# Bias and mask rows split on 80 partitions and stacked through a DRAM scratch, with the first tanh ahead of them

## The reference, cut to what matters

```
# 1 gated convolution, 7 taps, depthwise
gate = sigmoid(conv(x, gate_w) + gate_b);  cand = tanh(conv(x, cand_w) + cand_b)
h    = decay_scan(gate * cand);  y = h @ out_w.T + out_b + x;  y = rmsnorm(y) * norm_w
x    = layernorm(x + y)
# 2 cross attention, 16 heads of 8, causal, with an additive mask of the keys
wq = q @ Wq + bq;  wk = ctx @ Wk + bk;  wv = ctx @ Wv + bv
scores = where(causal, wq . wk / sqrt(8), min) + mask
x    = layernorm(x + softmax(scores) @ wv @ Wp + bp)
# 3 mixture of experts: gate, up and down, each routed to the top 2 of 8 experts
x    = layernorm(x + moe(silu(moe(x)) * moe(x)))
```

## Time and profile before

| | |
|---|---|
| time, median of 3 runs | 298.7 us (297.55 to 301.46) |
| the profiled execution's own time | 298.14 us |
| its span, first to last instruction | 296.4 us |
| mean granted TensorE clock | 0.936 |
| busy: PE, PEld, DVE, ACT, POOL | 257.1, 188.2, 190.8, 82.2, 111.1 us |
| mean DMA rate over the span | 79 GB/s |

### The profile page before, as it was taken

One profiled execution on the slowest core, in us unless ns is written; L12 is line 12 of the kernel. 1 busy time (PEld: TensorE's weight loads), 2 busy tenths in 40 slices (PEclk: granted clock), 3 DMA queues, 4 the chain that ended last, 5 costly groups with the idle time before them and its releaser, 6 DMA issues.

```text
span 296.4 us, 4809 instructions
## 1 busy us (share of the span) xinstructions
PE 257.1 (87%) x1756; PEld 188.2 (63%) x1756; DVE 190.8 (64%) x563; ACT 82.2 (28%) x157; POOL 111.1 (37%) x131
## 2 busy tenths in 40 slices
PE   6669857856986959999999999999999999999992
PEld 3546433425664737776777777777777787787871
DVE  5587862768697376556972884497188458566365
ACT  2424337135424201332133043114304313131000
POOL 4025329579314812048119205600930361070001
PEclk9997968995798885999999999999999999999997
DMA  5913625337420000262013005300300400320000
GB/s 192 380 50 112 197 75 148 116 106 214 160 71 1 3 0 0 109 209 77 0 48 107 2 0 170 125 0 13 142 2 1 155 0 2 71 81 9 2 0 18
DMA packets 12982, 23.48 MB, mean 79 GB/s; under 512 B 1584, under 2 KB 7824, under 8 KB 12954
## 3 DMA queue, kind: packets, MB, share of 16 engines
q1 hardware_dynamic: 11950, 22.17, 22.5%
q10 hardware_dynamic: 1008, 1.01, 1.0%
HBM read 19.81 MB, written 4.42 MB: 82 GB/s over the span
## 4 chain that ended last, share of the span: by engine, by line
PE 44%; DVE 31%; issue 12%; POOL 7%; ACT 3%; DMA 2%; SPq 1%; POOLq 0%; DVEq 0%; ACTq 0%
PE PS L1115 19%; PE PS L1167 8%; DVE NM L1321 4%; DVE ROOM L1454 3%; PE PS L1036 3%; PE PS L1047 2%; DMA PT<-aux 2%; DVE XL L1403 2%; PE PS L1050 2%; POOL PT L665 2%; DVE WL L1209 2%; PE PS L1010 2%; PE PS L881 2%; PE PS L1005 1%; PE PS L1089 1%
## 5 line engine op out<-in xcount | busy, mean ns | idle before, releaser
L1115 PE MATMUL PS<-WH,XH 128*128 128x512 f32 x128 | 57.8, 452 | 0.0
L1115 PE MATMUL PS<-WL,XH 128*128 128x512 f32 x128 | 52.2, 408 | 0.0
L1115 PE MATMUL PS<-WH,XL 128*128 128x512 f32 x128 | 52.2, 408 | 0.0
L689 POOL TENSOR_TENSOR ROOM<-ROOM,X2T 128x512 f32<-128x512 f32 x24 | 31.3, 1335 | 10.3 <-DMA ROOM<-CGD 10.3
L665 POOL TENSOR_SCALAR_AFFINE_SELECT PT<-PT 128x1024 f32<-128x1024 f32 x16 | 18.4, 1147 | 31.3 <-ACT PT L796 31.3
L1115 PEld LDWEIGHTS PS<-WH,XL 128*128 128x128 f32 x128 | 25.0, 196 | 6.1
L1115 PEld LDWEIGHTS PS<-WH,XH 128*128 128x128 f32 x128 | 25.1, 196 | 5.4 <-issue 0.4
L1115 PEld LDWEIGHTS PS<-WL,XH 128*128 128x128 f32 x128 | 25.2, 197 | 3.5 <-issue 0.2
L1167 PE MATMUL PS<-WH,ITH 128*128 128x512 f32 x56 | 23.7, 423 | 0.0
L607 POOL TENSOR_SCALAR R<-M 128x1 f32<-128x1 f32 x8 | 1.5, 190 | 58.0 <-DVE M L1467 58.0
L881 PE MATMUL PS<-XT,DIAG 128*128 128x256 f32 (+1 forms) x56 | 22.3, 538 | 0.0
(11 more groups left out here) (182 smaller groups left out, 491.8 us busy)
## 6 DMA issues: line engine op xcount, KB each, us to landing
ROOM<-CGD SPq DMA_DIRECT2D x12, 512.0 KB, 4.4
ROOM<-w_gate SPq DMA_DIRECT2D x4, 512.0 KB, 8.1
ROOM<-w_up SPq DMA_DIRECT2D x4, 512.0 KB, 4.5
ROOM<-w_down SPq DMA_DIRECT2D x4, 512.0 KB, 4.5
KD<-LOW SPq DMA_DIRECT2D x6, 256.0 KB, 4.4
KS<-KD SPq DMA_DIRECT2D x3, 512.0 KB, 3.6
QS<-QD SPq DMA_DIRECT2D x3, 512.0 KB, 4.5
QD<-LOW SPq DMA_DIRECT2D x3, 256.0 KB, 3.8
```

Of the source, the lines that this page charges most:

```text
L689: g.tensor_tensor(cb, cb, X2T[:, None, :].broadcast_to([P, 4, P]), ALU.mult).then_inc(f_xe, 1)
L1115: last = mm(PS[:, product_bank(t, r), :], a[:, r, cut], w[:, r, e * I:(e + 1) * I], start=e == 0 and n == 0, stop=e == E - 1 and n == 2)
```

## The change

The five rows are folded: 2048 columns are 16 pieces of 128, so 5 rows become 80 partitions of 128 columns. SP loads them so, now third, ahead of RO. ScalarE makes two results of 80 partitions by 128 columns (the scaled rows, and their low parts, with the choice of rows in the scale column), VectorE subtracts once. SP's new first step AX stores the result to the DRAM tensor AD, waits for the store, and loads the first 1280 columns of its five rows into AUX. K 0 waits for that load. VectorE's MX is gone, and SP's MX copies the masks from AD to MD, in DRAM. ScalarE's and VectorE's lists have GT 0 ahead of AX.

```diff
-C_AM = C_AW + 1
-C_BK, C_BQ = C_AM + 1, C_AM + 2
+C_BK, C_BQ = C_AW + 1, C_AW + 2
+A_FOLD = (A_T + M_COLS) // P
...
+        AD = nc.dram_tensor("AD", (A_ROWS, A_FOLD * P), F32, kind="Internal").ap()
...
-        AUX_RAW = PT[0:A_ROWS, :, :, :].rearrange("p a b c -> p (a b c)")
-        AUX_LOW = XH[0:A_ROWS, :, :].rearrange("p a b -> p (a b)")
-        MASKS = XL[0:A_ROWS, 0, :]
+        FOLD_RAW, FOLD_ALL = PT[0:A_ROWS * A_FOLD, 0, 0, :], PT[0:A_ROWS * A_FOLD, 0, 1, :]
+        FOLD_LOW, FOLD = XH[0:A_ROWS * A_FOLD, 0, 0:P], XH[0:A_ROWS * A_FOLD, 0, P:2 * P]
...
+            sp.dma_start(FOLD_RAW, aux.rearrange("a (c j) -> (a c) j", j=P)).then_inc(ld_a, 16)
             sp.dma_start(RO[:, :], rows.partition_broadcast(P)).then_inc(ld_r, 16)
-            sp.dma_start(AUX_RAW, aux).then_inc(ld_a, 16)
...
+                elif what == "AX":
+                    sp.wait_ge(c_aux, 3)
+                    sp.dma_start(AD.rearrange("a (c j) -> (a c) j", j=P), FOLD.bitcast(F32)).then_inc(st_a, 16)
+                    sp.wait_ge(st_a, 16)
+                    sp.wait_ge(c_id, 6)
+                    sp.dma_start(AUX[0:A_ROWS, :].bitcast(F32), AD[:, 0:A_COLS]).then_inc(ld_aux, 16)
                 elif what == "MX":
-                    sp.wait_ge(c_aux, 5)
-                    sp.dma_start(MD[0:2], MASKS[3:5, :].bitcast(F32)).then_inc(st_m, 16)
-                    sp.dma_start(MD[2:4], MASKS[0:2, :].bitcast(F32)).then_inc(st_m, 16)
+                    sp.wait_ge(c_id, 6)
+                    sp.dma_start(MD[0:2], AD[3:5, A_T:]).then_inc(st_m, 16)
+                    sp.dma_start(MD[2:4], AD[0:2, A_T:]).then_inc(st_m, 16)
...
-                    aux_q = AUX_RAW[:, A_Q:A_T]
-                    s.activation(aux_q, aux_q, ACT.Copy, scale=CO[0:A_ROWS, C_AS:C_AS + 1]).then_inc(c_aux, 1)
-                    s.activation(AUX_LOW[:, A_T:A_T + M_COLS], AUX_RAW[:, A_T:A_T + M_COLS], ACT.Copy,
-                                 scale=CO[0:A_ROWS, C_AM:C_AM + 1]).then_inc(c_aux, 1)
-                    act.wait_ge(c_aux, 1)
-                    s.activation(AUX_LOW[:, 0:A_T], AUX_RAW[:, 0:A_T], ACT.Copy,
-                                 scale=CO[0:A_ROWS, C_AW:C_AW + 1]).then_inc(c_aux, 1)
+                    s.activation(FOLD_ALL, FOLD_RAW, ACT.Copy, scale=CO[0:A_ROWS * A_FOLD, C_AS:C_AS + 1])\
+                        .then_inc(c_aux, 1)
+                    s.activation(FOLD_LOW, FOLD_RAW, ACT.Copy, scale=CO[0:A_ROWS * A_FOLD, C_AW:C_AW + 1])\
+                        .then_inc(c_aux, 1)
...
                         pe.wait_ge(ld_k, NLK)
-                        pe.wait_ge(c_aux, 4)
+                        pe.wait_ge(ld_aux, 16)
...
-                    dve.wait_ge(c_aux, 3)
-                    dve.wait_ge(c_id, 6)
-                    v.tensor_tensor(AUX[0:A_ROWS, :], AUX_RAW[:, 0:A_COLS], AUX_LOW[:, 0:A_COLS].bitcast(F32), ALU.subtract)\
-                        .then_inc(c_aux, 1)
-                elif what == "MX":
-                    dve.wait_ge(c_aux, 4)
-                    v.tensor_tensor(MASKS, AUX_RAW[:, A_T:A_T + M_COLS], AUX_LOW[:, A_T:A_T + M_COLS].bitcast(F32),
-                                    ALU.subtract).then_inc(c_aux, 1)
+                    dve.wait_ge(c_aux, 2)
+                    v.tensor_tensor(FOLD, FOLD_ALL, FOLD_LOW.bitcast(F32), ALU.subtract).then_inc(c_aux, 1)
...
+    row_of, part = np.arange(P) // A_FOLD, np.arange(P) % A_FOLD * P
+    scales = np.where((row_of < 2) & (part >= A_Q) & (part < A_T), np.float32(SCALE), np.float32(1))
+    lows = (row_of == np.where(part < A_T, 1, 4)).astype(np.float32)
...
+        scales[:, None], (scales * lows)[:, None],
```

More of the change, by code:

```diff
@@ L61 @@
 MASK_HI, MASK_LO, MAX_HI, MAX_LO = range(COPIES - 1, 4 * COPIES, COPIES)
-EARLY = {'PE': [('WM', 4), ('WM', 1), ('WM', 1), ('GC', 0), ('GC', 1), ('O', 0), ('C1', 0), ('KN', 0), ('K', 0), ('X1', 0), ('C1', 1), ('V', 0), ('KN', 1), ('Q', 0), ('V', 1), ('C1', 2), ('S', 0, 0), ('O', 1), ('S', 0, 1), ('C1', 3), ('C1', 4), ('A', 0), ('X1', 1), ('ST', 0, 0), ('ST', 0, 1), ('C1', 5), ('C1', 6), ('PV', 0, 0), ('C1', 7), ('PV', 0, 1), ('WO', 0), ('S', 1, 0), ('C1', 8), ('C1', 9), ('X2', 0), ('QN', 0), ('LG', 0), ('C1', 10), ('C1', 11), ('C1', 12), ('C1', 13), ('S', 1, 1), ('T', 0), ('T', 1), ('A', 1)], 'ACT': [('AX',), ('GT', 0), ('O', 0), ('KE', 0), ('X1', 0), ('KN', 0), ('W', 0), ('GT', 1), ('QE', 0), ('W', 1), ('KN', 1), ('O', 1), ('X1', 1), ('W', 2), ('W', 3), ('ST', 0, 0), ('ST', 0, 1), ('DC',), ('W', 4), ('W', 6), ('X2', 0), ('LG', 0), ('QN', 0), ('W', 5), ('T', 0), ('T', 1), ('W', 7)], 'DVE': [('GC', 0), ('AX',), ('GT', 0), ('GC', 1, 0), ('GC', 1, 1), ('O', 0), ('GC', 1, 2), ('QW',), ('GC', 1, 3), ('N1', 0), ('N1A', 0), ('GC', 1, 4), ('GC', 1, 5), ('GC', 1, 6), ('N1B', 0), ('KE', 0), ('KN', 0), ('GT', 1), ('V', 0), ('MX',), ('QE', 0), ('KN', 1), ('WL', 1, 0), ('O', 1), ('S', 0, 0), ('S', 0, 1), ('N1', 1), ('N1A', 1), ('V', 1), ('NM', 0), ('A', 0), ('N1B', 1), ('WL', 1, 1), ('RD',), ('WL', 3, 1), ('WL', 3, 0), ('PV', 0, 1), ('WO', 0), ('N2', 0), ('S', 1, 0), ('LG', 0), ('WL', 5, 1), ('T', 0), ('QN', 0), ('S', 1, 1), ('NM', 1), ('A', 1), ('T', 1)], 'POOL': [('GT', 0), ('N1', 0), ('N1B', 0), ('WL', 0, 0), ('GT', 1), ('WL', 0, 1), ('VM', 0), ('N1', 1), ('N1B', 1), ('WL', 2, 1), ('X1', 0), ('WL', 2, 0), ('ST', 0, 0), ('X1', 1), ('ST', 0, 1), ('WL', 4, 1), ('N2', 0), ('WL', 6, 0), ('WL', 6, 1), ('WL', 4, 0), ('XE', 0), ('XE', 1), ('XE', 2), ('WL', 5, 0), ('XE', 3), ('WL', 7, 1), ('VM', 1), ('WL', 7, 0)], 'SP': [('KN', 0), ('W', 0), ('MX',), ('MS',), ('W', 1), ('W', 3), ('W', 2), ('KN', 1), ('W', 4), ('QN', 0), ('W', 5), ('W', 6)]}
@@ new lines @@
+EARLY = {'PE': [('WM', 4), ('WM', 1), ('WM', 1), ('GC', 0), ('GC', 1), ('O', 0), ('C1', 0), ('KN', 0), ('K', 0), ('X1', 0), ('C1', 1), ('V', 0), ('KN', 1), ('Q', 0), ('V', 1), ('C1', 2), ('S', 0, 0), ('O', 1), ('S', 0, 1), ('C1', 3), ('C1', 4), ('A', 0), ('X1', 1), ('ST', 0, 0), ('ST', 0, 1), ('C1', 5), ('C1', 6), ('PV', 0, 0), ('C1', 7), ('PV', 0, 1), ('WO', 0), ('S', 1, 0), ('C1', 8), ('C1', 9), ('X2', 0), ('QN', 0), ('LG', 0), ('C1', 10), ('C1', 11), ('C1', 12), ('C1', 13), ('S', 1, 1), ('T', 0), ('T', 1), ('A', 1)], 'ACT': [('GT', 0), ('AX',), ('O', 0), ('KE', 0), ('X1', 0), ('KN', 0), ('W', 0), ('GT', 1), ('QE', 0), ('W', 1), ('KN', 1), ('O', 1), ('X1', 1), ('W', 2), ('W', 3), ('ST', 0, 0), ('ST', 0, 1), ('DC',), ('W', 4), ('W', 6), ('X2', 0), ('LG', 0), ('QN', 0), ('W', 5), ('T', 0), ('T', 1), ('W', 7)], 'DVE': [('GC', 0), ('GT', 0), ('AX',), ('GC', 1, 0), ('GC', 1, 1), ('O', 0), ('GC', 1, 2), ('QW',), ('GC', 1, 3), ('N1', 0), ('N1A', 0), ('GC', 1, 4), ('GC', 1, 5), ('GC', 1, 6), ('N1B', 0), ('KE', 0), ('KN', 0), ('GT', 1), ('V', 0), ('QE', 0), ('KN', 1), ('WL', 1, 0), ('O', 1), ('S', 0, 0), ('S', 0, 1), ('N1', 1), ('N1A', 1), ('V', 1), ('NM', 0), ('A', 0), ('N1B', 1), ('WL', 1, 1), ('RD',), ('WL', 3, 1), ('WL', 3, 0), ('PV', 0, 1), ('WO', 0), ('N2', 0), ('S', 1, 0), ('LG', 0), ('WL', 5, 1), ('T', 0), ('QN', 0), ('S', 1, 1), ('NM', 1), ('A', 1), ('T', 1)], 'POOL': [('GT', 0), ('N1', 0), ('N1B', 0), ('WL', 0, 0), ('GT', 1), ('WL', 0, 1), ('VM', 0), ('N1', 1), ('N1B', 1), ('WL', 2, 1), ('X1', 0), ('WL', 2, 0), ('ST', 0, 0), ('X1', 1), ('ST', 0, 1), ('WL', 4, 1), ('N2', 0), ('WL', 6, 0), ('WL', 6, 1), ('WL', 4, 0), ('XE', 0), ('XE', 1), ('XE', 2), ('WL', 5, 0), ('XE', 3), ('WL', 7, 1), ('VM', 1), ('WL', 7, 0)], 'SP': [('AX',), ('KN', 0), ('W', 0), ('MX',), ('MS',), ('W', 1), ('W', 3), ('W', 2), ('KN', 1), ('W', 4), ('QN', 0), ('W', 5), ('W', 6)]}
@@ L323, in decoder_layer @@
         c_aux = sem("c_aux")
+        st_a = sem("st_a")
+        ld_aux = sem("ld_aux")
         dv = sem("dv")
@@ L1504 @@
         marks(*range(2, 32, COPIES)), marks(*range(1, 32, COPIES), MASK_LO),
-        np.where(np.arange(P) < 2, np.float32(SCALE), np.float32(1))[:, None],
-        (np.arange(P) == 1).astype(np.float32)[:, None],
-        (np.arange(P) == 4).astype(np.float32)[:, None],
+        scales[:, None], (scales * lows)[:, None],
         a["L0_xattn_bk"][:, None], a["L0_xattn_bq"][:, None]], axis=1)
```

## The result

The changed kernel takes 300.58 us (median of 20 runs, 298.33 to 303.87) where the kernel before, in 20 runs beside them, takes 300.38 (295.76 to 303.34). The ratio is 1.0089, with a 95% interval of 1.0051 to 1.0128: slower by 0.9%. This ratio leaves out the runs more than 1.5% above the fastest of their kernel, 11 of the 20 before and 5 of the 20 after; the means of all 20 are 299.72 and 301.18 us, 0.5% apart (0.1 to 0.9%). So the runs show that the change costs time, and its size only as somewhere between 0.1 and 1.3%. The profiled execution took 299.41 us, span 297.7, against 298.14 and 296.4 before. Two repeats gave 1.0066 (1.0026 to 1.0107), and a median of 301.95 against 300.9. The means of all runs of the three comparisons together, 40 of the changed kernel and 52 of the kernel before, put the cost at 1.6 us, give or take 0.8.

The account below looks back on a forecast made before the run. The prediction took the chain of waits to belong to TensorE for 44% and VectorE for 31%, transfers 2%. Terms of +3.5, -0.6 and -0.3 gave +2.6 on the profiled 298.14: 300.7 us, range 295.6 to 303.0.

Parts of the forecast that it names:

- GT 0 ahead: At the head, the first tanh starts at about 8.5 us, O 0 runs 2.6 us earlier, norms end 2.7 earlier.
- Work on 80 partitions: Two ScalarE operations of 0.3 us and a VectorE one of about 0.3; result ready for the store at 10.9.
- The round trip: Store and reload ahead of K 0: store waits behind weight loads, seen at 17.5, AUX lands at 19.5 us.
- the estimate of 20.2: End of store and reload in us, at about 2.0 us fixed per transfer; not the figure the forecast used.
- The clock in K 0: After TensorE's idle stretch K 0 starts at 1.2 GHz and takes 4.7 us, where it took 2.79.
- the +3.5: Lateness in us of KS, behind K 0's copy: 1.6 for the late AUX and 1.9 for the clock.
- KN 1 and MX: Between KS and QS: KN 1 falls behind the clock's return, -0.6 us; dropping MX on VectorE gains 0.3.
- QS +2.6: QS, and with it S 0 0 and everything behind, comes 2.6 us later than in the kernel before.
- A shift of the early steps should pass to the end almost whole: Past 9.2 us nothing on the chain waits for a transfer and each step hangs on the one before.
- The sum: From K 0's copy to the end: +3.5, -0.6 and -0.3 us give +2.6, so 300.7 us.
- rival 5: The clock pattern moves: a low stretch falls on the expert matmuls, another 2 to 3 us, 303; chance 0.08.
- Two per cent is [...] about what a measurement of this kernel can tell from no change: Whole kernel: 2% is 6.0 us, which no case reaches; chance of within 2% 0.94, slower 0.04, faster 0.02.

Follow-up runs that it names:

- own_queue: The changed kernel with store and reload issued by ScalarE on its own queue; median 301.69 us, against 300.9 for the kernel before.
- late_weights: The changed kernel with the three first 512 KB weight loads issued behind the reload of AUX; 295.68 us, in a repeat 295.99 us, ratio 0.9888 to the kernel before.
- keep_warm: The changed kernel with ten matmuls that nobody reads ahead of K 0 on TensorE; median 300.74 us, against 300.9 for the kernel before.
- mx_back: The changed kernel with an unread 5 x 1024 subtraction on VectorE at MX's old place; 302.19 us, ratio 1.0117 to the kernel before.
- shift_1: The kernel before with one more subtraction ahead of MX on VectorE; 304.55 us, ratio 1.0186 to the kernel before.
- before_late: The kernel before with the three first weight loads held back until AUX is written; 298.12 us, ratio 0.9943 to the kernel before.
- second_trip: The changed kernel with one more DRAM copy between store and reload; 302.62 us, ratio 1.0152 to the kernel before.

## Why the prediction was right and wrong

**GT 0 ahead: right.** Tanh at 8.61 (8.5), O 0 at 13.01 in this trace and 11.72 in the second repeat (11.85), residual at 13.66 and 12.36 (12.7), norm's end at 20.25 and 18.95 (19.2). The first trace is later because TensorE's taps took 634 ns each up to about 8 us and 378 behind; in the trace of before all but the first took 378.

**Work on 80 partitions: right in cost, early in time.** 0.39, 0.39 and 0.26, for 0.3 each. The result was ready for the store at 12.1, 11.7 and 11.5 in the three traces, not at 10.9: in the first two the second tanh waited for slower taps, and in the third the scans ended at 11.25, not at 10.6. The weight loads ahead covered that, so it cost nothing.

**The round trip: right.** Store seen at 17.36 (17.5), AUX in at 19.57 (19.5). By what it waits for, own_queue corrects the words: not SP's queue but the engines behind both queues. The 2.0 us fixed per transfer of the Trainium skill, "DMA: Bandwidth & Descriptors", section "Anatomy of one DMA — SWDGE (gpsimd) path", from which the estimate of 20.2 came, is nearer for the reload (2.21, and 2.1 from issue to K 0 in late_weights) than for the store (1.5 and 1.8 in the two traces of late_weights).

**The clock in K 0: right in kind, and the split of the +3.5 off.** K 0 took 4.6 us for 4.7. But the 2.79 us that were scaled up held 0.43 us of weight load ahead of the first matmul, which the wait for AUX now hides; from the first matmul it was 2.4, and the low clock made 4.6 of it. So the late AUX is worth 1.4, not 1.6 (keep_warm's 3.6 us from the start of K 0 to KS, put behind 19.71, against 21.92), and the clock 2.2, not 1.9. That 3.6 came out for 3.5 is two errors that cancel. Nor is the clock's part a constant: from the start of K 0 to KS it is 5.8, 4.8 and 5.3 us in the three traces of the changed kernel, so the term lies between 1.2 and 2.2, with a mean of 1.7. The smaller terms, with starts of K 0 0.2 later and 0.3 earlier than in the first trace, make the +1.9 and +1.8 of the repeats.

**KN 1 and MX: right.** -0.6 for KN 1 at the returned clock and -0.3 for MX gave -0.9; measured is -1.0 (8.42 from KS to QS before, 7.47 after). The copy of Q 0 is ready 8.15 us behind KS before and 7.43 after, so KN 1's part is -0.7. The two can't be priced alone: with MX in place the earlier copy is worth nothing, and once the copy is early MX is worth the whole 1.0, by VectorE's list in mx_back.

**QS +2.6: right for the first trace (+2.6), 0.7 and 0.8 too much for the repeats.** The mean of the three is 2.1.

**"A shift of the early steps should pass to the end almost whole": the step that failed.** The sum gives the clock behind QS nothing; it stands only in rival 5, with 0.08, and there it can only add. The runs show it as the ordinary case, of both signs. From QS to the last landmark the three traces of the changed kernel go from +2.6, +1.9, +1.8 to +1.2, +4.2, +3.4; at tile 1, near the first expert matmuls, where the prediction wanted the same shift, they have +2.7, +5.3, +3.3. Runs of one kernel spread over 5.5 (changed) and 7.6 us (before). And shift_1 shows that +2.7 at QS can cost 1.9%, 5.6 us, twice its length, when a low stretch comes with it. That the changed kernel's cost, 1.6 us by all runs and 2.0 to 2.7 by the ratios, is near its mean shift of 2.1 is thus no proof of the rule. In all three of its traces the clock is at 1.00 from 26 to 40 us, over the scores, as in the kernel before up to 40. A likely reason is that its wait took the place of one that was there: its low stretch, 19 to 25 us, stands for the one at 22.95 to 26.3. No run tests that.

**"Two per cent is [...] about what a measurement of this kernel can tell from no change": wrong too, and with it the forecast of no change to be told.** With the forecast and its rivals inside the 2%, no change to be told carried 0.94. Twenty runs of each told 0.9% (0.5 to 1.3) from none, and by the means of all of them 0.5% (0.1 to 0.9): slower, clear of noise, by less than half of what the text thought could be told. By the forecast's own cases slower by less than 2% was the likeliest, and that part stands.

**The level: luck in part.** 300.7 was forecast and 300.58 measured. But the kernel before measured 300.38 in 20 runs, not 298.7 in three. Against 298.7 the forecast was a rise of 2.0, 0.7%; against the 20 runs it is one of 0.3, while +2.6 on 300.38 would have been 303.0. The median of the changed kernel's 20 runs came out low beside its mean, 301.18.

**What is open:** the size of the cost between 0.1 and 1.3%; why before_late is 0.6% down with QS in place, if it is; why the store of second_trip came early; and where the low stretches past 50 us fall, which no kernel here controls.

## What to carry to other kernels

Look at what is in flight before counting a small transfer as cheap. Store and reload through DRAM took 3.6 and 4.0 us alone, and 7.5 to 8.2 behind 1.5 MB of prefetch (from the issue of the store to the start of K 0 or the landing of AUX), and another queue did not help. So put prefetches that nobody needs soon behind the round trip (1.1% faster than the kernel before). Before pricing a stall at its length, look at what TensorE's clock does behind it: here one that fell where a low stretch already was cost about its length or less, and one with a new stretch behind it cost twice its length. Take a term's size from several executions where the clock has a part in it.

## What the runs showed of the hardware

- Two queues, one backlog. On ScalarE's queue, which had nothing else, the 40 KB store took 16.73 - 11.46 = 5.3 us while SP's weight loads ran. The Trainium skill, "DMA: Bandwidth & Descriptors", section "Queues, rings and completion order", says that a semaphore increment lands only after every earlier write of that DMA engine, across its queues. The trace agrees, but doesn't tell whether the data of the store or only its semaphore waited.
- The granted clock can read 1.00 where matmuls run slow. In the changed kernel the taps of 256 columns took 634 ns from 5.4 to about 8 us and 378 after, with 1.00 in all windows there. K 0's projections, also of 256 columns, took a median of 634 ns at 0.50 (379 before, at 1.00), so TensorE was in all likelihood at 1.2 GHz until 8 us. At the start of a trace read the durations, not that column.
- VectorE and GpSimd can hold each other up: GpSimd's VM (L657, L666) takes 2.20 us beside a 5 x 1024 subtraction that starts just before it and 1.30 in the changed kernel without it. In shift_1 the first subtraction, ahead of VM, takes 1.20, and the second, which starts while VM runs, 2.19.
